# One instruction block for routing and experts, earlier first normalisation of two groups, own banks for the last group, blank rows one step later

## What is computed

```python
h = take(weight, x)                                   # 32 x 128 x 256
X = layernorm(h)
q, k, v = X @ q_w, X @ k_w, X @ v_w                   # 16 heads
scores = where(causal, q k^T / 4, -inf)
h = h + softmax(scores) v @ o_w
X = layernorm(h)
scores = softmax(X @ wg); top1 = argmax(scores)       # 8 experts
rank = position of the token among those of its expert; valid = rank < capacity
y = gelu(rows_of_expert @ W1 + b1) @ W2 + b2
out = h + where(valid, y[slot], 0) * combine_weight
```

## Time and profile before

| | us |
|---|---|
| time, median of three runs | 623.44 |
| profiled execution | 626.09 |
| its span in the trace | 624.4 |
| start of the first product of expert 0 | 366.57 |

### The profile page before, as it was taken

One profiled execution on the slowest core, in us unless ns is written; L12 is line 12 of the kernel. 1 busy time (PEld: TensorE's weight loads), 2 busy tenths in 40 slices (PEclk: granted clock), 3 DMA queues, 4 the chain that ended last, 5 costly groups with the idle time before them and its releaser, 6 DMA issues. The chain is left out here.

```text
span 624.4 us, 14332 instructions
## 1 busy us (share of the span) xinstructions
PE 576.3 (92%) x5311; PEld 498.5 (80%) x5371; DVE 419.6 (67%) x1073; ACT 338.8 (54%) x708; POOL 258.3 (41%) x316
## 2 busy tenths in 40 slices
PE   6778899989999999999898799999999999999993
PEld 3466677877877877787665369999999999999993
DVE  6255678988898888888766266565656575757531
ACT  2233555555555556555462168585858585858550
POOL 5445777765556655565563200404030403040303
PEclk9897999999999999999999999999999999999997
DMA  4678777546786644556111132151515151511101
GB/s 124 202 245 282 239 224 227 160 147 225 230 252 212 194 149 135 157 161 222 35 36 69 45 115 98 35 180 39 179 35 180 33 180 35 177 36 45 33 2 32
DMA packets 42581, 84.39 MB, mean 135 GB/s; under 512 B 6822, under 2 KB 32987, under 8 KB 38864
## 3 DMA queue, kind: packets, MB, share of 16 engines
q1 hardware_dynamic: 35600, 70.66, 35.6%
q0 software_dynamic: 6144, 12.67, 6.4%
q10 hardware_dynamic: 768, 0.13, 0.1%
HBM read 52.64 MB, written 31.74 MB: 135 GB/s over the span
## 5 line engine op out<-in xcount | busy, mean ns | idle before, releaser
L1009 POOL DMA_INDIRECT out_dram<-ys,xs x48 | 50.1, 1045 | 218.6 <-DVE ys L1206 209.1
L400 POOL TENSOR_SCALAR_AFFINE_SELECT pt<-pt 128x512 f32<-128x512 f32 x128 | 81.9, 640 | 86.0 <-ACT pt L442 84.5
L442 ACT ACTIVATE pt<-C 128x512 f32<-128x512 f32 x128 | 76.5, 598 | 72.1 <-PE C L616 68.1
L1219 DVE TENSOR_TENSOR hl<-gl,hh 128x324 fp32r<-128x324 f32 x128 | 63.3, 495 | 38.7 <-ACT hh L1049 34.1
L796 DVE TENSOR_REDUCE mx<-S 128x4 f32<-128x512 f32 x128 | 86.7, 681 | 4.0 <-PE S L602 2.2
L1049 ACT ACTIVATE hh<-gl 128x324 fp32r<-128x324 f32 x128 | 61.7, 491 | 0.0
L602 PE MATMUL S<-ks,qs 96*128 96x128 bf16 x512 | 50.2, 220 | 8.6 <-issue 6.6
L715 PE MATMUL PV<-pt,va 128*32 128x128 f32 x1024 | 54.1, 284 | 1.6 <-ACT os L449 0.8
L602 PEld LDWEIGHTS S<-ks,qs 96*128 96x128 bf16 x512 | 40.1, 98 | 15.7 <-issue 0.6
L616 PE MATMUL C<-qs,ks 97*128 97x128 bf16 x512 | 50.3, 220 | 1.0 <-DMA qs<-nm 1.0
L1206 DVE SCALAR_TENSOR_TENSOR ys<-C,xs 108x256 f32<-108x256 f32 x48 | 21.8, 481 | 40.1 <-PE C L1099 36.9
(11 more groups left out here) (157 smaller groups left out, 1706.8 us busy)
## 6 DMA issues: line engine op xcount, KB each, us to landing
w_raw<-in_L_ffn_W_dram SPq DMA_DIRECT2D x16, 1024.0 KB, 8.7
qs<-q_parts SPq DMA_DIRECT2D x48, 256.0 KB
ks<-k_parts SPq DMA_DIRECT2D x48, 256.0 KB
q_parts<-qp SPq DMA_DIRECT2D x16, 384.0 KB, 2.4
k_parts<-kp SPq DMA_DIRECT2D x16, 384.0 KB
rows_of_slots<-w_raw SPq DMA_DIRECT2D x6, 877.5 KB
xs<-rows_of_slots SPq DMA_DIRECT2D x8, 658.1 KB
out_dram<-h SPq DMA_DIRECT2D x16, 256.0 KB
```

What stands on the lines that cost most here:

```text
L400: pool.affine_select(out=buf[:, :, :], in_=buf[:, :, :], compare_op=ALU.is_ge, fill=0.0, base=0, pattern=[[0, 4], [1, S]], channel_multipl ...
L442: act.activation(pt[u % 4][:, :, :], bC[u % 2][:, :].rearrange("p (j t) -> p j t", j=4), ACT.Exp, scale=SCALE).then_inc(a_exp, 1)
L1009: pool.indirect_dma_start(out=outf, out_offset=bass.IndirectOffsetOnAxis(ap=xs[e.slot][:, j, D + 3:D + 4].bitcast(U32), axis=0), in_=ys[j] ...
L1219: dve.tensor_tensor(hl[:, f, cols], gl[u % 4][:, :], hh[:, f, cols].bitcast(F32), ALU.subtract).then_inc(v_hl, 1)
```

## The change

The two phases return functions for each engine, and one block runs both in turn, so that no engine waits for the others between them. SP waits for the rows' stores at the head of the expert part, loads the rows of expert 0 in three DMAs with semaphores of their own, and then those of expert 1. ACT enters the expert part when the last places are known (`v_pos`), since the buffers of the experts lie over those of attention; `h` and `pos`, still in use then, lie under `hh` and `hl`. DVE splits all eight pieces of the weights of expert 0 before the rows. The first normalisation of groups 1 and 2 is at the head of steps 0 and 1. The last group (15) has its second normalisation at the end of step 19, its transpose there at s = 7 in bank C0, and its logits in bank C1. The blank rows begin in step 1; step 5 sends two. The numbers of filling matmuls differ.

```diff
+        block = whole.enter_context(nc.Block())
+        @block.sync
+        def _(sp):
+            routing["sync"](sp)
+            experts["sync"](sp)
...
+        def final(g):
+            return g.off == NG - 1
+        def turn_bank(g):
+            return bC[0] if final(g) else bM2
+        def logit_bank(g):
+            return bC[1] if final(g) else bM2
...
-                if i < BLANKS:
-                    if i == 0:
-                        sp.wait_ge(v_blank, 2)
-                    sp.dma_start(slots[:, :].rearrange("(p a m) c -> p a (m c)", p=96, a=BLANKS)[:, i], blank
-                                 ).then_inc(d_init, 16)
+                if i == 1:
+                    sp.wait_ge(v_blank, 2)
+                for c in range(BLANKS):
+                    if i == min(c + 1, BLANKS - 1):
+                        sp.dma_start(slots[:, :].rearrange("(p a m) c -> p a (m c)", p=96, a=BLANKS)[:, c], blank
+                                     ).then_inc(d_init, 16)
...
-            for i in range(2):
-                sp.wait_ge(d_slot[i], 16 * NG)
-            sp.wait_ge(d_rows, 16 * NG)
...
-                    if g and s == 5:
+                    if g and s == (0 if i < 2 else 5):
                         wait(pool, v_ve1, g.times(1, 1))
                         pool.tensor_tensor(rs1[:, :], ve1[:, :], halfneg[:, 0:GB], ALU.pow).then_inc(p_rs1, 1)
...
                 if g5:
-                    from_bank(x2t, bM2, pe_x2T, g5, a_x2t)
+                    if final(g5):
+                        wait(act, pe_lg, g5.times(1))
+                    from_bank(x2t, turn_bank(g5), pe_x2T, g5, a_x2t)
...
-            FILL = {(1, 1): 6, (1, 4): 8, (NG + 3, 1): 2, (NG + 3, 3): 3, (NG + 3, 5): 6, (NG + 3, 6): 3,
-                    (NG + 4, 1): 4, (NG + 4, 5): 4, (NG + 4, 6): 3, (NG + 5, 1): 4}
+            FILL = {(1, 1): 6, (1, 4): 18, (NG + 3, 1): 4, (NG + 3, 3): 3, (NG + 3, 5): 6, (NG + 3, 6): 3,
+                    (NG + 3, 7): 6, (NG + 4, 1): 2, (NG + 4, 6): 2, (NG + 5, 1): 4}
...
                     if g and s == 7:
+                        if g.off == 1:
+                            idle_work(bPV, 3)
                         wait(pe, v_xn, g.times(1, 1))
-                        if g.off == 1:
-                            idle_work(bPV, 14)
...
-                    if g and s == 5:
+                    if g and s == 5 and not final(g):
...
+                    g = group(n, i - 4)
+                    if g and s == 7 and final(g):
+                        wait(pe, v_xn2, g.times(1, 1))
+                        wait(pe, a_exp, UNITS * NG)
+                        turn4(turn_bank(g), xn2).then_inc(pe_x2T, 1)
...
-            idle_work(bS[0], 32)
+            idle_work(bS[0], 44)
...
+                if i < 2:
+                    stats1(nxt)
+                    norm1(nxt)
                 maxima(0)
...
-                if not g4:
+                if not g4 and g5 and not final(g5):
                     second_norm(g5)
...
-                if nxt:
+                if nxt and i > 1:
                     stats1(nxt)
...
-                if nxt:
+                if nxt and i > 1:
                     norm1(nxt)
...
                 maxima(7)
+                if g4 and final(g4):
+                    wait(dve, pe_x2T, g4.times(1))
+                    second_norm(g4)
                 if g5:
                     route(g5)
...
-            load_rows(expert(0, 0))
+            sp.wait_ge(d_rows, 16 * NG)
+            for i in range(2):
+                sp.wait_ge(d_slot[i], 16 * NG)
+            rows_of = slots[0:SL, :].rearrange("(p j) c -> p j c", j=NT)
+            for r in range(TURNS):
+                sp.dma_start(xs[0][:, 2 * r:2 * r + 2, :], rows_of[:, 2 * r:2 * r + 2, :]).then_inc(d_first[r], 16)
             load_rows(expert(0, 1))
-
-            sp.wait_ge(d_xs[0], 16)
...
+            act.wait_ge(v_pos, NG)
             e0 = expert(0, 0)
...
-            idle_work(22)
             for r in range(TURNS - 1):
                 turn(expert(0, 0), r)
-                idle_work(5)
+            idle_work(6)
...
-            for c in range(PIECES // 2):
+            for c in range(PIECES):
                 split(e0, c)
-            normalise(e0, 0)
-            normalise(e0, 1)
-            normalise(e0, 2)
+            for j in range(4):
+                normalise(e0, j)
             turned(e0, 0)
-            normalise(e0, 3)
-            turned(e0, 1)
             normalise(e0, 4)
             normalise(e0, 5)
-            split(e0, 4)
+            turned(e0, 1)
             turned(e0, 2)
-            for c in (5, 6, 7):
-                split(e0, c)
```

More of the change, by code:

```diff
@@ L125, in lm_block @@
         d_raw = [sem(f"d_raw{q}") for q in range(2)]
+        d_rows, d_slot, v_pos = sem("d_rows"), [sem(f"d_slot{i}") for i in range(2)], sem("v_pos")
         def load_w1(eng, e, q):
@@ L137, in lm_block, with _ @@
         load_half = (load_w1, load_w2)
-        attention_phase(nc, sb_in, sem, locals())
-        expert_phase(nc, sb_in, sem, locals())
+        routing = attention_phase(nc, sb_in, sem, locals())
+        experts = expert_phase(nc, sb_in, sem, locals())
+        block = whole.enter_context(nc.Block())
[3 more added lines that the diff above has]
+            experts["sync"](sp)
+        @block.gpsimd
+        def _(pool):
+            routing["gpsimd"](pool)
+            experts["gpsimd"](pool)
+        @block.scalar
+        def _(act):
+            routing["scalar"](act)
+            experts["scalar"](act)
+        @block.tensor
+        def _(pe):
+            routing["tensor"](pe)
+            experts["tensor"](pe)
+        @block.vector
+        def _(dve):
+            routing["vector"](dve)
+            experts["vector"](dve)
 def attention_phase(nc, sb_in, sem, v):
@@ L160, in attention_phase @@
         sb = sb_in(scope)
+        h = sb("h", [P, NB, ROW], F32)
+        pos = [sb(f"pos{i}", [P, GB], U32) for i in range(2)]
         identb = sb("identb", [P, P], BF16)
@@ L229, in attention_phase @@
         d_sh = [sem(f"d_sh{i}") for i in range(RING)]
-        d_rows, d_slot = sem("d_rows"), [sem(f"d_slot{i}") for i in range(2)]
+        d_rows, d_slot, v_pos = v["d_rows"], v["d_slot"], v["v_pos"]
         g_set, g_cst, v_cst = sem("g_set"), sem("g_cst"), sem("v_cst")
@@ L424, in _, with scalar @@
             steps(pool, step)
-        @block.scalar
-        def _(act):
+        def scalar(act):
             for m in range(4):
@@ L513, in _, with tensor @@
             steps(act, step)
-        @block.tensor
-        def _(pe):
+        def tensor(pe):
             def turn4(dst, src):
@@ L719, in _, with vector @@
             steps(pe, step)
-            idle_work(bS[0], 32)
-        @block.vector
-        def _(dve):
+            idle_work(bS[0], 44)
+        def vector(dve):
             dve.wait_ge(d_x, 16)
@@ L957, in expert_phase @@
         d_xs = [sem(f"d_xs{q}") for q in range(2)]
+        d_first = [sem(f"d_first{r}") for r in range(TURNS)]
         d_out = [sem(f"d_out{j}") for j in range(NT)]
@@ L970, in steps, with sync @@
                 step(0, i)
-        block = scope.enter_context(nc.Block())
-        @block.sync
-        def _(sp):
+        def sync(sp):
             def load_rows(e):
@@ L1000, in _, with gpsimd @@
                 sp.wait_ge(d_out[j], 16 * E)
-        @block.gpsimd
-        def _(pool):
+        def gpsimd(pool):
             def step(n, i):
@@ L1173, in normalise @@
                 rows_of = xs[e.slot]
-                wait(dve, d_xs[e.slot], e.round(16, 16))
+                if e.off == 0:
+                    dve.wait_ge(d_first[j // 2], 16)
+                wait(dve, d_xs[e.slot], e.round(16, 16) if e.slot else e.round(16))
                 wait(dve, e_turn, e.times(TURNS))
```

25 lines of the change are left out of this document (11 added, 14 removed).

## The result

Timed side by side, the changed kernel takes 620.0 us (median of four runs, 619.5 to 621.5), the kernel before 623.5 us (four runs): a ratio of 0.9927, 95% interval 0.9903 to 0.9951. It is 0.6 to 0.7% faster, about 4 us, where 10.3 were forecast. The profiled execution has a span of 619.6 us, 4.8 less than before (the three others have 617.6 to 618.2). Both profiled executions are slower than the medians: 621.5 against 620.0 us after, 626.09 against 623.5 before.

What follows compares the result with a forecast made beforehand. PE was taken to bound the kernel, in steady attention and from the first expert product to the end, with waits in start-up and handover. Gains of 3.9 + 6.4 = 10.3 us off the 623.44 median gave 613.1 us, range 609.8 to 616.6.

Steps and rivals of the forecast that it cites:

- start-up: Steps 0 to 2: earlier normalisation brings the first C forward, the latest of three queues deciding, 3.9 us gained.
- DVE behind POOL: Start-up, head of step 1: DVE waits for POOL's power behind four gathers; `qr` of group 1 still 3.8 us earlier.
- The loads of group 0: Start-up: stacked loads take 9 to 9.8 us from issue at 22.1, landing at 31 to 32, 2.5 to 3.3 us earlier.
- The loads of group 1: Start-up: issued 3.8 us earlier at 33.2, landing 9.8 us later at 43.0; first C at 48.0, 3.9 us earlier.
- rival (a): Start-up: PE works sparsely, the clock falls to half speed and 2 to 2.5 us are lost, 615.4 us; chance 0.16.
- (c): Start-up keeps nothing, as DMA engines bound group 1's loads; only the handover gain is left, 617.0 us; chance 0.08.
- The last group: Group 15, end of attention: its logits start at 344.2 instead of 344.69 and the last store moves along, 0.5 us gained.
- The handover: Between attention and experts: no meeting, rows in three loads; first product 6.4 us earlier, 0.5 of it from the last group.
- rival (e): Handover: PE or ACT comes late to the expert part, or the weight split lasts longer; 615.6 us with 2.5 us; chance 0.06.
- The blanks: Blank rows sent one step later, two in step 5: costed at nothing, at most 2.7 us if ahead of a load.
- Rival (b): Start-up: more is kept, as the clock does not fall at 48 or stacked loads land sooner; 610.3 us; chance 0.12.
- Rival (d): Steps 1 to 5: PE starves for loads and stays at 1.2 GHz; slower, 627.6 us with five stretches; chance 0.03.

Runs made afterwards that it cites:

- e1: The changed kernel plus one POOL drain at the head of POOL's expert part: 618.44 us, ratio 0.9845 to the kernel before.
- e6: The changed kernel plus a POOL drain at the head of each expert's POOL part: 616.27 us, ratio 0.9821 to the kernel before.
- e8: The changed kernel plus one POOL drain at the head of step 16 of attention: 621.95 us, ratio 0.9914 to the kernel before.
- e2: The changed kernel with the old start-up (first normalisations, filling matmuls, blank rows in their old places): 625.23 us, ratio 0.9948 to the kernel before.
- e3: The changed kernel with step 0's gathers of token rows issued in step 1 instead: 623.38 us, ratio 0.9915 to the kernel before.
- e5: The changed kernel plus a POOL drain before the expert part, and one gather group per step from step 1, none in step 0: 612.77 us, ratio 0.9755.
- e11: The changed kernel with one gather group per step from step 1 and a POOL drain at each expert's head: 611.51 us, ratio 0.978 to the kernel before.
- e4: The changed kernel with the blank rows back in steps 0 to 5, one each: 622.83 us, ratio 0.9911 to the kernel before.
- e12: The kernel before with one edit, one group of gathers per step from step 1 and none in step 0: 624.78 us, ratio 0.9992.

## Why the prediction was wrong

The time was forecast at 613.1 us, with 609.8 to 616.6 as its range; it is 620.0. The missing 6.9 us lie in two places.

**The step that failed first: "whatever moves the first product of expert 0 moves the end by as much".** It was read from the chain, which ends in PE. But the program ends in the closing meeting of the engines, and that waits for POOL's drain. The prediction names the meeting at the end of the first block as 3.7 us that fall away, without asking who came last there. It was POOL's drain. The 3.7 us did fall away at the handover, but the drain at the end of the program now has 112 indirect DMAs behind it and not 48 and lasts 3.1 us longer, and the last indirect DMAs come 0.65 us late. The sum had these 3.75 us at nothing, and none of the rivals has them. e1, e6 and e8 show it.

**The second: start-up, 3.9 us forecast, 0.8 to 1.3 measured (e2), which can't be told from nothing.** By its own three queues:

- *DVE behind POOL*: right. Power done at 26.8, normalisation from 26.85, `qr` of group 1 at 27.50, where 27.4, 28.15 and 28.1 stood.
- *The loads of group 0*: wrong. 9 to 9.8 us were taken from group 1's loads; they took 13.1. The prediction noted that the gathers "now start some 0.5 us earlier" and used it only for POOL. In the trace SP's transfers move 1.28 MB in the 7 us in which they had moved 1.70. e3, e5 and e11, without these gathers, have the first score at 31.8, 30.9 and 32.4, where 31 to 32 was forecast. Whether their earlier start or the first parts of group 1, which SP now sends from 30.1, weighs more was not tried apart.
- *The loads of group 1*: issued at 35.55, not 33.2. They read what SP has just sent to DRAM, and SP waits for that send of `q_parts`, issued at 30.11 while the loads of group 0 were under way. It was assumed to take as long as before, where the wait was 0.2 us. SP's wait in the start-up, before and after:

```profile
SPq L301 <- DMA q_parts<-qp: 0.2, 1, 0.2
SPq L336 <- DMA q_parts<-qp: 3.2, 1, 3.2
```

- *The clock*: PE waited, 1.75 busy in 6 us, and then ran at 1.2 GHz from 33.4 to 40.2. By the prediction's own sign, a half-clock stretch between 30 and 40, this is rival (a), given 0.16.

So two rivals came true together: (a), and (c), the start keeps nothing because the DMA engines are the limit, given 0.08. (c) has its own signs in the late loads and sends, with the engines at 0.99, and what was said against it, loads issued 15 us apart of which a group needs under 10, failed: they are now 13.7 us apart (21.84, 35.55), and group 0 took 13.1. What each of the two cost was not separated.

With the start-up at 0.8 to 1.3 us instead of 3.9 and the end at 3.75 instead of nothing, 6.4 to 6.9 us of the 6.9 are accounted for.

**The last group**: 0.5 us forecast. From the power to the logits it is 3.18 us, before 3.82: 0.64. At the last store 0.36 are left (9.20 against 9.56), and the last two stores take 1.37 and 1.50 us on POOL where the last took 0.98 before. DVE's weight split now runs beside them; whether it is the cause was not tried.

**The handover**: 6.4 us forecast with the last group's 0.5; 6.2 in the profiled pair, 6.6 to 6.9 in those of e1 to e4 (19.1 to 18.85 us against 25.7; the same stretch of the kernel before is 26.5 in e12, so about 1 us is the spread of single traces). Its steps: the wait of the stores 13.5 us (13.0 before) and no other wait after it; first tiles 3.09 us after the issue (3.3 forecast); from there to the first product 3.8 (4.05). PE and the split were not late, so rival (e) is out.

**The blanks**: at nothing, and e4 can't be told from the change. **Rival (b)**, more is kept, didn't come; e5 shows that it was to be had with another edit. **Rival (d)**, slower: the half clock stayed with two stretches, and the steady part is untouched.

## What to carry over

A closing meeting of engines has a last comer too: when a change removes a meeting, look at who was late there and for what, since the work (here POOL's drain) may only move to the end. When one chain is made earlier in a start-up in which the DMA engines are at 0.9 or more, its transfers meet those that used to run beside it; count the bytes ahead of the first load, and move what isn't needed yet together with the edit. Two edits that each bring about nothing can bring some 4 us together, so try the pair before dropping either.

## What the runs showed of the hardware

- POOL's drain grows with the indirect DMAs started since its last drain: 1.9 us beyond the last of them after 6, 4.0 after 48, 5.0 after 60, 5.3 after 64, 7.1 after 112. Drains where no engine waits for POOL (e1, e6) made the last one short at no visible cost; the one in the middle of attention (e8) took 6.2 us and delayed PE.
- Without a drain between the phases the last indirect DMA starts 253.2 to 253.3 us after the first product in all five traces of such kernels, and 252.5 to 252.6 in the eight with one (e8's in step 16) and the full clock; in the change only the last four are late.
- TensorE's half-clock stretches in the start-up last 3.4 or 6.8 us, and where they fall differs with small shifts of the start: e2's profiled run has a single one of 3.4, e3's four. e5 and e11 have the same start-up and differ by 2.9 us at the first C.
- Executions of one kernel differ with the mean granted clock: of the 19 of the kernel before in the set e5 to e8, the fastest, 623.88 us, has 0.991, the slowest, 630.27, has 0.977. A trace is of one execution; look at its time and clock beside the others before reading differences of 2 or 3 us from it.
